# Softmax reciprocals by a power on GpSimd in a fused cross-attention and ternary-FFN kernel

## What is computed

```
x = x + attention(layernorm(x), context)      # 16 heads; scores = q k^T, softmax over 64 keys
x = x + ffn(layernorm(x))                     # two ternary-weight linear layers with 8-bit activations, gelu between
attn = softmax(scores);  ctx_c = attn @ kv_rope;  out = project(ctx_c)
```

## Time and profile before

| | us |
|---|---|
| Median of 2 runs | 469.84 |
| The two runs | 467.57, 472.11 |
| Span of the profiled execution | 470.1 |
| PE busy in that span | 399.1 (85%) |
| DVE busy | 344.6 (73%) |
| ACT busy | 257.7 (55%) |
| POOL busy | 218.9 (47%) |

### The profile page before, as it was taken

How to read it: one execution, slowest core, us unless ns; L and a number is a source line. 1 busy time by engine, 2 the same in 40 slices (tenths; PEclk the granted TensorE clock), 3 DMA queues, 4 the chain that set the end, 5 groups by cost and what they waited for, 6 DMA issues and landing times.

```text
span 470.1 us, 8743 instructions
## 1 busy us (share of the span) xinstructions
PE 399.1 (85%) x2775; PEld 277.9 (59%) x2775; DVE 344.6 (73%) x909; ACT 257.7 (55%) x472; POOL 218.9 (47%) x269
## 2 busy tenths in 40 slices
PE   0998887989789897999999999999999997776463
PEld 0465754667557573767676767676767674464221
DVE  1805654788978896978787878787878788977663
ACT  0223244534276854676858585858485858555430
POOL 1000001445455474465655646474747474857551
PEclk9999998999899998999999999999999999999765
DMA  8950436431212323243425252434345343444435
GB/s 272 350 159 20 205 120 199 135 92 48 57 47 59 82 69 82 62 106 74 108 65 114 59 115 64 107 82 93 81 92 83 91 97 77 104 125 79 100 67 91
DMA packets 65085, 48.55 MB, mean 103 GB/s; under 512 B 51216, under 2 KB 56592, under 8 KB 64016
## 3 DMA queue, kind: packets, MB, share of 16 engines
q1 hardware_dynamic: 62656, 41.70, 36.4%
q10 hardware_dynamic: 2384, 6.29, 4.0%
HBM read 31.72 MB, written 4.46 MB: 77 GB/s over the span
## 4 chain that ended last, share of the span: by engine, by line
issue 41%; POOL 36%; PE 5%; DMA 3%; DVE 2%; POOLq 1%; SPq 1%; ACT 0%; DVEq 0%
POOL cl L529 10%; POOL tq L550 7%; POOL qb L553 6%; POOL yc L537 3%; POOL xa L542 3%; POOL xn L293 3%; POOL xq L545 3%; DMA qt<-qb 1%; DMA rinv_d<-ri 1%; DMA rb<-rinv_d 1%; POOLq L184 1%; PE hps L778 1%; PE ps L692 1%; PE ps L694 1%; PE hps L708 1%
## 5 line engine op out<-in xcount | busy, mean ns | idle before, releaser
L529 POOL TENSOR_TENSOR cl<-cr,ch 128x512 fp32r<-128x512 f32 x64 | 83.4, 1325 | 166.3 <-ACT ch L602 166.3
L692 PE MATMUL ps<-xh,ah 128*128 128x256 f32 x256 | 75.6, 295 | 7.1 <-ACT g L617 4.5
L746 PE MATMUL hps<-bh,ch 128*128 128x256 f32 x256 | 75.8, 296 | 1.3 <-POOL cl L529 1.3
L586 ACT ACTIVATE qf<-ps 128x512 f32<-128x512 f32 x64 | 37.5, 586 | 68.0 <-PE ps L694 68.0
L694 PE MATMUL ps<-xh,al 128*128 128x256 f32 x256 | 72.4, 283 | 0.0
L693 PE MATMUL ps<-xl,ah 128*128 128x256 f32 x256 | 72.3, 282 | 0.0
L748 PE MATMUL hps<-bh,cl 128*128 128x256 f32 x256 | 71.5, 279 | 0.0
L747 PE MATMUL hps<-bl,ch 128*128 128x256 f32 x256 | 71.4, 279 | 0.0
L602 ACT ACTIVATE ch<-cr 128x512 fp32r<-128x512 f32 x64 | 39.3, 631 | 56.8 <-DVE cr L866 56.8
L692 PEld LDWEIGHTS ps<-xh,ah 128*128 128x128 f32 x256 | 49.2, 192 | 29.2 <-issue 28.7
L778 PE MATMUL hps<-w2q,qt 128*128 128x256 bf16 x256 | 37.4, 295 | 19.8 <-DMA qt<-qb 15.1
(11 more groups left out here) (129 smaller groups left out, 812.3 us busy)
## 6 DMA issues: line engine op xcount, KB each, us to landing
rb<-rinv_d SPq DMA_DIRECT2D x64, 256.0 KB, 4.0
out<-yo SPq DMA_DIRECT2D x32, 128.0 KB, 3.8
wq_s<-wq ACTq DMA_DIRECT2D x2, 1024.0 KB, 12.1
wo_s<-wo_t SPq DMA_DIRECT2D x1, 2048.0 KB, 9.0
w_s<-w_t SPq DMA_DIRECT2D x2, 1024.0 KB, 5.3
xs<-x SPq DMA_DIRECT2D x2, 1024.0 KB, 5.0
xs<-x ACTq DMA_DIRECT2D x1, 1536.0 KB, 14.6
wk_a<-wk_t ACTq DMA_DIRECT2D x2, 512.0 KB, 9.2
```

Source lines behind the costliest of these rows:

```text
L529: pool.tensor_tensor(cl[:, u % 2, :, b * S:(b + 1) * S], cr[:, :, b * S:(b + 1) * S], ch[:, u % 2, :, b * S:(b + 1) * S].bitcast(F32), ALU ...
L692: pe.matmul(o, ah[:, c, cols], xh[:, k % 2, c, :], start=(c == 0), stop=False)
L746: pe.matmul(O[:, 0:D], c_h, bh[:, hp, :], start=(hp == 0), stop=False)
```

## The change

The sums and the maxima change places in `red` and in T: maxima on partitions 64 to 95, sums on partitions 0 to 31. `row_sum` on DVE is now the reduction alone. The reciprocal is a new function `row_inverse` on POOL: one two-input instruction that raises the 32x64 sums to the power of a tile `minus` filled with -1. It stands in step n, for tile n-1, ahead of `ctx_lo` of tile n-2. The semaphore `rinv_steps` becomes two, `row_sums` (DVE) and `row_inverses` (POOL); `row_sum` also waits until the inverse of two tiles before is done. The diff, cut:

```diff
+                pool.memset(minus[:, :], -1.0).then_inc(sem["eps_set"], 1)
...
                 def shift_rows(u):
-                                     nmax[:, p, 32 * gg:32 * gg + 32].bitcast(F32)).then_inc(sem[f"shift_rows{p}"], 16)
+                                     nmax[64:96, p, 32 * gg:32 * gg + 32].bitcast(F32)).then_inc(sem[f"shift_rows{p}"], 16)
                 def rinv_rows(u):
-                    sp.wait_ge(sem["rinv_steps"], 2 * u + 2)
+                    sp.wait_ge(sem["row_inverses"], u + 1)
-                                     ri[64 + 16 * b:64 + 16 * b + 16, p, :].rearrange("k (g s) -> k g s", s=32)).then_inc(sem[f"rinv_stored{p}"], 16)
+                                     ri[16 * b:16 * b + 16, p, :].rearrange("k (g s) -> k g s", s=32)).then_inc(sem[f"rinv_stored{p}"], 16)
...
+                def row_inverse(u):
+                    hi = slice(0, 32)
+                    pool.wait_ge(sem["row_sums"], u + 1)
+                    at_least(pool, sem[f"rinv_stored{u % 2}"], 32 * (u // 2))
+                    pool.tensor_tensor(ri[hi, u % 2, :], rs[hi, u % 2, :], minus[hi, :], ALU.pow).then_inc(sem["row_inverses"], 1)
...
                     if n % 2 and tile(n - 9):
                         g_round(n - 9)
+                    if tile(n - 1):
+                        row_inverse(n - 1)
                     if tile(n - 2):
                         ctx_lo(n - 2, 0)
...
                 def turned(u):
-                    at_least(pe, sem["rinv_steps"], 2 * (u - 2) + 1)
+                    at_least(pe, sem["row_sums"], u - 1)
...
                 def row_sum(u):
-                    hi = slice(64, 96)
+                    hi = slice(0, 32)
                     dve.wait_ge(sem["red_turned"], u + 2)
+                    at_least(dve, sem["row_inverses"], u - 1)
                     dve.tensor_reduce(rs[hi, u % 2, :].rearrange("p (g s) -> p g s", s=32),
-                                      T[hi, 0:P].rearrange("p (g a s) -> p g s a", g=2, a=2), AX.X, ALU.add).then_inc(sem["rinv_steps"], 1)
-                    dve.wait_ge(sem["rinv_steps"], 2 * u + 1)
-                    at_least(dve, sem[f"rinv_stored{u % 2}"], 32 * (u // 2))
-                    dve.reciprocal(ri[hi, u % 2, :], rs[hi, u % 2, :]).then_inc(sem["rinv_steps"], 1)
+                                      T[hi, 0:P].rearrange("p (g a s) -> p g s a", g=2, a=2), AX.X, ALU.add).then_inc(sem["row_sums"], 1)
```

## The result

The changed kernel takes 694.49 us (2 runs, 693.37 to 695.61) against 469.84: a ratio of 1.4745, with a 95% interval of 1.4675 to 1.4815. The prediction was 465.0, in a range from 460.5 to 488. Its rival A had the direction, and nothing had the size.

The account below looks back on a forecast made before the run. PE was taken as the bound in the steady part. 470.1 - 5.9 (shorter PE waits) + 0.6 (step 1) + 0.5 (tail) = 465.3 us of span, so 465.0 us predicted; range 460.5 to 488.

Parts of the forecast that it names:

- rival A: POOL's power takes over 3.8 us, so PE waits for norm_x; about 487 us at 4.5, 500 at 5; chance 0.26.
- the length of the power: POOL's power on the 32x64 sums, called D: taken as 2.0 us, between bounds of 0.26 and 5.4.
- What hides D: POOL's power fits into room in POOL's queue in even and odd steps, so at 2.0 us it is hidden there.
- D may be 3.8 us before PE stands still: Even step: norm_x's result has 1.75 us of room, so POOL's power may last 3.8 us without delaying PE.
- The sentence on SP's transposing DMAs: Odd step: x_round ends by 256.0, and SP's two 2.5 us DMAs still end before shift_rows at 260.5, so hidden.
- B: Rival: power of 2.8 to 3.8 us; step 1, step 3 and tail eat the gain; 467 to 471 us; chance 0.16.
- The reciprocal leaves DVE: On DVE, divide follows row_sum directly, gaining 0.69 us; PE's ten 0.46 us waits for xl vanish; gelu wait stays.
- 5.9 us: PE's total gain: 4.6 from ten xl waits, 0.69 from the long wait at 181.53, 0.6 from the shift DMA wait.
- Rival C: DVE's time counts everywhere: 449 us if all 31 steps gave 0.69, otherwise about 457; chance 0.08.
- Two places have less cover: POOL's power delays SP's stores of the reciprocals: step 1 pays 0.6 us, and 0.5 us of the tail reach the end.
- behind the power it may wait until 250.97 or for one L529 more: DVE's two-input L882 may be held by POOL, harmless since quadrant_sum behind it waits for ACT until 252.55 anyway.
- The waits for nothing: row_sum's added wait for the inverse of two tiles before, and the moved maxima and sums with their DMAs, cost nothing.

Follow-up runs that it names:

- the chain opened: Changed kernel with DVE's x_max behind residual and PE's turned ahead of both halves of project: 653.57 us, ratio 1.3855.
- the product: Changed kernel with a plain product (sums times 0.05) in place of POOL's power, division left out: 464.51 us, ratio 0.9853.
- 8 columns: Changed kernel with the power on 8 of the 64 columns and a product on the other 56: 469.87 us, ratio 0.9991.
- the later reciprocal: Reciprocal on DVE behind divide and xl: 462.75 us with the changed kernel's places of sums and maxima, 467.58 us with those of the kernel before.
- 16 columns: Changed kernel with the power on 16 of the 64 columns and a product on the other 48: 478.35 us, ratio 1.0133.
- the new places alone: Changed kernel with the reciprocal back on DVE directly behind row_sum, sums and maxima still swapped: 468.12 us, ratio 0.9928.

## Why the prediction was wrong

**The step that failed is the length of the power**, "I take 2.0 us" between bounds of 0.26 and 5.4. It is 10.55. The upper bound counted 33 dependent steps at 2.5 ns an element at worst; the runs show some 160 ns an element, twice that. The kernel's own inverse square root runs on DVE and gave only a count of steps, L553 in the earlier trace rows says how long POOL's plain arithmetic takes, and neither says anything of how POOL makes a power. The argument against rival A, that 3.8 us would be "24 times that of L529" an element, took an odd price for an unlikely one: the real factor is 65. A bound from above was not to be had from these rows, and then "too long by any amount" should have held more than 0.26.

The Trainium skill, "GPSIMD Engine Reference", section 3, has POOL at 2.6 cycles for an element against DVE's 1, and at 1.96 times DVE's time for a measured addition, so the prediction's 2.6 was a ratio of cycles and not of times. The trace shows 19 times the reciprocal's 544 ns: the factor doesn't hold for a power. For plain arithmetic of this shape no run here shows it, since no product of it was run on DVE.

**What hides D** was wrong on its own. "D may be 3.8 us before PE stands still": at 3.2 the pair is already 22.85. Two chains were missed. The sentence on SP's transposing DMAs is about x_round's two (turn_x) in the even step; turn_g, which stands ahead of shift_rows in the odd step and waits for g_round, was not looked at, and it is what PE's wait hangs on at 3.2. And the closed chain over x_max, the norms and row_sum was not seen, because each link was followed for one step only, from row_sum to norm_x. Its sum, two powers and 15.9 us, was within reach: all its links stand in the trace of the kernel before.

**Rival A** was right in kind: L306 waits for norm_x and L738 for the shift DMA, as it said, and the slope is two us per us. But it lets this begin at 3.8 (at 3.2, where B had 467 to 471 us, 478.35 were measured), and where it says that POOL is the bound (12.3 us and two powers, 33.4 at D = 10.55), the changed kernel takes 37.0. POOL's work alone sets the time only with the chain opened.

**The reciprocal leaves DVE**: right in the pairs. The ten waits of 0.46 are gone, the pair is 0.46 us shorter, divide starts 0.08 before row_sum's end, and the gelu wait is unmoved at 4.5 us in 11 places, before and after. That "5.9 us" stands so near the 7.0 measured with the product is in part luck: step 12, with the long wait at 181.53, was booked with 0.69 us and gave 2.2, since the granted clock didn't fall there (last section). Rival C is gone by the times: it had 457 or less, the product gave 464.5, and 462.75 came with DVE's work all kept. By the Trainium skill, "VectorE: DVE Perf Modes", on two Vector instructions with no wait between them, a change of partition group holds the next one. The traces agree: row_sum starts 0.03 after row_max's end (64 to 0), divide 0.08 before row_sum's end (both from 0).

**"Two places have less cover"** was too small. The 0.6 and 0.5 us named there are the difference between 8 columns and the product in the prediction; measured it is 5.4 us (469.87 against 464.51). Step 1's 0.6 doesn't show (30.0 us from the first row_max to that of step 3, 30.2 with the product). What does is x_scale: "behind the power it may wait until 250.97 or for one L529 more" became 2.3 to 2.8 us in the odd steps of the loop, which is hidden, and 4.73 in step 5, which is not. Had D been 2.0, the time would have been about 470, not 465.

**The waits for nothing**: right. The inverse of two tiles before, the moved maxima and sums and their DMAs cost nothing in the kernel with the product.

## What to carry to other kernels

An operation that no row shows has no upper bound from its neighbours: time it alone, at two sizes, before moving it, and if that can't be done, let the chances say so. What was worth having here was the place in the queue and the partitions, not the busy time: the same reciprocal, on the same engine, behind divide and `xl`, gives as much as taking it off. When work goes into an in-order queue, look for closed chains over two engines' queues; their length grows by the added work once per step, whatever room a single step shows.

## What the runs showed that was not expected

**A power on GpSimd** takes 0.16 us for each element of a partition, on 32 or 128 partitions alike: 10.56 us for 64, 5.43 for 32, 2.9 for 16, 1.66 for 8.

**TensorE after a wait.** In the changed kernel the granted clock is 0.83 from 297 to 334 us; over 240 to 280 in the kernel before it is 1.00. PE's timeline after one of its waits:

```profile
330.22 0.58 PE L756 MATMUL hps<-bh,ch 128*128 128x256 f32 x1 [3.65 <-POOL cl L531]
330.60 0.41 PE L757 MATMUL hps<-bl,ch 128*128 128x256 f32 x1
330.81 0.41 PE L758 MATMUL hps<-bh,cl 128*128 128x256 f32 x1
...
333.63 0.28 PE L757 MATMUL hps<-bl,ch 128*128 128x256 f32 x1
333.74 0.28 PE L758 MATMUL hps<-bh,cl 128*128 128x256 f32 x1
```

For 2.8 us they follow each other at 0.21 us, at a granted clock of 0.50, the lower level (1.2 GHz); from 333.6 on at 0.12, at 1.00 (2.4 GHz). A wait costs more than its length by that. It is also in the small runs. Step 12 of each kernel has one wait of PE for `xl` (3.25 us in the kernel before). These are the stretches from its end to the start of the queries: window, length, busy PE, PEld, DVE, ACT, POOL, clock, DMA. They are the later reciprocal with the old places (a wait of 2.83 us ahead), with the new places (2.33), and the kernel with 16 columns (3.30):

```profile
178.68:186.02 7.34, 6.90 (x34) 2.48 (x33) 4.89 (x11) 4.78 (x8) 3.92 (x7) 0.77 0.56 135
...
179.39:185.31 5.92, 5.48 (x34) 2.05 (x35) 3.98 (x11) 4.87 (x8) 4.14 (x7) 1.00 0.52 111
...
182.79:188.71 5.92, 5.48 (x35) 2.06 (x35) 3.98 (x10) 4.87 (x8) 5.58 (x9) 1.00 0.45 100
```

The same work takes 7.3 to 7.6 us where the clock falls (the kernel before, the new places alone, 8 columns, and the first of these) and 5.9 where it doesn't. So 1.4 of the 1.7 us by which the new places are faster in step 12 are the clock. The wait's length alone doesn't decide it: the clock fell after 2.70 and 2.83 us, and not after 3.30. What decides it stays open, with one trace of each kernel.

**DVE beside POOL.** The two-input instruction of the earlier trace rows starts in the kernel before at 251.17, in the first half of ctx_lo, and ends with it at 251.76. In the kernel with the later reciprocal and the new places it starts at 247.01 and takes 0.19 us, for that half ends at 247.15. An instruction of the same kind and size (L893) takes 0.16 us in the kernel before, at 265.32, just as ctx_lo ends. So the time above that is a wait for POOL, and it is not always for one instruction: in the kernel with 8 columns it outlasts two halves, centre and the weight instruction, 4.73 us. Why the first half's end frees it in one kernel and not in the other is open.
